# A graph kernel on one core: one of eight edge selections built on POOL, table and weight work cut into more pieces, the last empty half round dropped

## The reference, cut to what matters

```python
col = edge_index[1]
agg = jax.ops.segment_sum(edge_attr, col, num_segments=x.shape[0])
h = jnp.concatenate([x, agg], axis=-1)
h = jax.nn.relu(h @ W1 + b1)
h = jax.nn.relu(h @ W2 + b2)
h = h @ W3 + b3
...
deg = jax.ops.segment_sum(jnp.ones_like(src, dtype=x.dtype), src, num_segments=n)
```

## Time and profile before

| | us |
|---|---|
| median of 3 runs (2772.12 to 2778.86) | 2774.24 |
| the profiled execution's own time | 2776.76 |
| its span | 2775.0 |
| PE busy over the span | 2137.8 |
| DVE busy | 1990.9 |
| ACT busy | 1713.1 |
| POOL busy | 1795.3 |
| mean granted TensorE clock | 0.922 of full speed |

### The profile page before, as it was taken

How to read it: one execution, slowest core, us unless ns; L and a number is a source line. 1 busy time by engine, 2 the same in 40 slices (tenths; PEclk the granted TensorE clock), 3 DMA queues, 4 the chain that set the end, 5 groups by cost and what they waited for, 6 DMA issues and landing times. The chain is left out here.

```text
span 2775.0 us, 60619 instructions
## 1 busy us (share of the span) xinstructions
PE 2137.8 (77%) x13885; PEld 1762.5 (64%) x13886; DVE 1990.9 (72%) x7056; ACT 1713.1 (62%) x4484; POOL 1795.3 (65%) x1900
## 2 busy tenths in 40 slices
PE   6989977766787788788787876677788777777776
PEld 6988933254666676676676654566566666666655
DVE  7888868756777777777787855666676666676664
ACT  5766656455566666666676635556666666666663
POOL 1240055477777777777777726777777777777773
PEclk9999978689999989999999987999999999999998
DMA  6776623233334433434434413333333333333332
GB/s 185 237 243 184 205 65 110 89 103 105 110 112 117 119 113 116 119 114 117 118 112 120 117 56 97 107 109 111 107 113 111 106 110 110 108 110 110 106 113 59
DMA packets 183239, 331.21 MB, mean 119 GB/s; under 512 B 39636, under 2 KB 94887, under 8 KB 182964
## 3 DMA queue, kind: packets, MB, share of 16 engines
q0 software_dynamic: 82704, 223.04, 28.1%
q1 hardware_dynamic: 99524, 104.49, 12.3%
q10 hardware_dynamic: 736, 0.93, 0.1%
HBM read 295.96 MB, written 20.71 MB: 114 GB/s over the span
## 5 line engine op out<-in xcount | busy, mean ns | idle before, releaser
L1827 POOL DMA_INDIRECT arena<-kv_rows,idx_stage x1664 | 1618.5, 973 | 574.7 <-issue 498.4
L1915 PE MATMUL bank<-arena 128*128 128x136 f32 x3328 | 601.0, 313 | 315.5 <-DVE aggregate L1954 314.6
L1915 PEld LDWEIGHTS bank<-arena 128*128 128x128 f32 x3328 | 474.2, 204 | 423.5 <-DVE aggregate L1954 304.0
L1954 DVE TENSOR_TENSOR aggregate<-bank,aggregate 128x136 f32 x1664 | 489.5, 294 | 198.6 <-issue 99.0
L1906 PE MATMUL bank<-queries,arena 128*128 x3328 | 489.8, 294 | 133.1 <-DVE arena L1982 131.9
L1906 PEld LDWEIGHTS bank<-queries,arena 128*128 128x128 f32 x3328 | 437.0, 205 | 170.9 <-issue 170.3
L1982 DVE TENSOR_TENSOR arena<-bank,arena 128x512 f32<-128x512 f32 x416 | 286.4, 688 | 352.0 <-DMA arena<-kv_rows,idx_stage 278.3
L1848 ACT ACTIVATE arena<-iota_n,at_negdst 128x128 f32<-128x128 f32 x1664 | 527.4, 394 | 3.9 <-DMA queries<-arena 2.1
L1872 ACT ACTIVATE arena<-arena 128x32 f32<-128x32 f32 x416 | 93.6, 225 | 486.6 <-DVE arena L2012 304.7
L1891 PE MATMUL bank<-ident,arena 128*128 128x128 f32 x1664 | 273.6, 290 | 68.5 <-issue 37.2
L1962 DVE TENSOR_TENSOR arena<-arena 128x512 f32<-128x512 f32 x416 | 284.3, 683 | 46.1 <-ACT arena L1872 45.5
(11 more groups left out here) (279 smaller groups left out, 2699.4 us busy)
## 6 DMA issues: line engine op xcount, KB each, us to landing
arena<-in_edge_attr_dram SPq DMA_DIRECT2D x248, 256.0 KB, 3.2
arena<-kv_rows,idx_stage POOLq DMA_INDIRECT x1664
kv_rows<-arena SPq DMA_DIRECT2D x12, 512.0 KB, 3.8
kv_rows<-arena SPq DMA_DIRECT2D x24, 256.0 KB, 2.1
arena<-in_x_dram SPq DMA_DIRECT2D x12, 256.0 KB, 4.0
x_rows<-arena SPq DMA_DIRECT2D x12, 256.0 KB, 3.1
x_stream<-arena SPq DMA_DIRECT2D x12, 256.0 KB, 2.3
queries<-arena SPq DMA_DIRECT2D x12, 256.0 KB, 2.7
```

Source lines behind the costliest of these rows:

```text
L1827: pool.indirect_dma_start(kv[:, n, :], None, kv_dram[l], bass.IndirectOffsetOnAxis(idx_stage[:, half % 2, n:n + 1], 0)).then_inc(Z.kv_in[s ...
L1915: pe.matmul(sums_of(j), sel[:, r % SEL_SLOTS, j, :], msg[:, r % 2, j, :], start=True, stop=True).then_inc(Z.sum, 1)
L1954: dve.tensor_tensor(a, sums_of(j), a, ALU.add).then_inc(Z.added, 1)
```

## The change

Four edits. (1) Slot 0 of every odd round is selected by POOL, with four `tensor_scalar` is_equal of 128x128 in place of DVE's one 128x512; DVE keeps slots 0 and 1 of even rounds and slot 1 of odd rounds, ACT keeps slots 2 and 3. PE waits for `es_sel_pool` there. (2) Stops stand before each of the bodies 2 to 28. The step marks go to bodies 4 and 5, the tiles to 7, the ordering is halved (13, 14), the weight pieces go to 16, 18, 20, 22, their last part to 23, the table's parts to 24, 26, 28; PE's pieces to 3, 6, 12, 17, 19, 21, 25, 27. (3) POOL's loads and gathers are handed out over bodies 2 to 19, ahead of its selection for that body. (4) The last round (61) has no sums: 244 steps are done in 61 rounds; its counts stay.

```diff
-DVE_SLOTS = 2
-ACT_SLOTS = ES_SLOTS - DVE_SLOTS
+ES_DONE = ES_STEPS - ES_SLOTS
+assert ES_DONE >= ES_TILES + NT - 1
+POOL_ODD = 0
+DVE_SLOTS = ((0, 1), (1,))
+DVE_BODY = 3
+ACT_SLOTS = 2
+ACT_FIRST = ES_SLOTS - ACT_SLOTS
...
-        STOPS = tuple(range(3, 17, 2)) + tuple(range(17, 27))
+        STOPS = tuple(range(2, 29))
...
-                for n in range(2 * ES_SLOTS):
+                for n in range(ES_SLOTS if last else 2 * ES_SLOTS):
                     if not first:
                         sp.wait_ge(es_summed, (i - 1) * 2 * ES_SLOTS + n + 1)
...
+        def pool_edge_sums(pool):
+            pool.wait_ge(s_tab, 1)
+
+            def body(i):
+                m, s = i * 2 + 1, POOL_ODD
+                if i:
+                    pool.wait_ge(es_summed, (m - 2) * ES_SLOTS + s + 1)
+                for j in range(ES_SUB):
+                    one = pool.tensor_scalar(es_sel[:, 1, s, j, :], iota_n[:, :], es_dst[:, m * ES_SLOTS + s, j:j + 1], None, ALU.is_equal)
+                one.then_inc(es_sel_pool, 1)
+
+            def between(i):
+                if i == 2:
+                    pool_load_first(pool)
+                if i in range(3, 8):
+                    pool_load_layers(pool, i - 3)
+                if i == 8:
+                    pool_gather_rows(pool, AT, range(0, 4))
+                if i == 9:
+                    pool_gather_rows(pool, AT, range(4, AT.step_chunks))
+                if i in range(10, 15):
+                    pool_load_layers(pool, i - 5)
+                if i == 12:
+                    pool_write_pairs(pool)
+                if i == 15:
+                    pool_gather_pairs(pool, range(0, 4))
+                if i == 16:
+                    pool_gather_pairs(pool, range(4, AT.step_chunks))
+                if i == 18:
+                    pool_gather_in_order(pool, range(0, 4))
+                if i == 19:
+                    pool_gather_in_order(pool, range(4, AT.step_chunks))
+            for i in range(ES_BODIES - 1):
+                between(i)
+                body(i)
...
-                    for s in range(ES_SLOTS):
+                    for s in range(0 if last_body and h == 1 else ES_SLOTS):
                         pe.wait_ge(es_in[h * ES_SLOTS + s], 16 * (i + 1))
-                        if s < DVE_SLOTS:
-                            pe.wait_ge(es_sel_dve, m * DVE_SLOTS + s + 1)
+                        if h == 1 and s == POOL_ODD:
+                            pe.wait_ge(es_sel_pool, i + 1)
+                        elif s in DVE_SLOTS[h]:
+                            pe.wait_ge(es_sel_dve, i * DVE_BODY + h * len(DVE_SLOTS[0]) + DVE_SLOTS[h].index(s) + 1)
...
-                for h in range(2):
-                    m, ahead = i * 2 + h, not (last and h == 1)
...
+                for h in range(1 if last else 2):
+                    m = i * 2 + h
...
                     add(m, h, 1)
-                    for s in range(2):
-                        if ahead and s < DVE_SLOTS:
-                            select(m + 1, 1 - h, s)
-                        add(m, h, 2 + s)
+                    ahead = () if last else DVE_SLOTS[1 - h]
+                    for s in range(2, ES_SLOTS):
+                        if s - 2 < len(ahead):
+                            select(m + 1, 1 - h, ahead[s - 2])
+                        add(m, h, s)
...
-                if n == 1:
-                    dve_done(dve, AT)
...
+                if i == 4:
+                    dve_done(dve, AT, 0, 4)
+                if i == 5:
+                    dve_done(dve, AT, 4, AT.chunks)
...
+                if i in (13, 14):
+                    dve_order_steps(dve, i - 13)
+                if i in (16, 18, 20, 22):
+                    dve_weights(dve, (i - 16) // 2)
+                if i == 23:
+                    dve_weights(dve, 4)
+                if i in (24, 26, 28):
+                    dve_attention_table(dve, (i - 24) // 2)
...
-            sp.wait_ge(es_added, ES_STEPS)
+            sp.wait_ge(es_added, ES_DONE)
```

More of the change, by code:

```diff
@@ L438, in pool_load_weights @@
                           (rows_l[l][:, 1, :], w["b2"].partition_broadcast(P))]
-                for o, i in loads:
-                    pool.dma_start(o, i).then_inc(s_wl, 16)
+            n = -(-len(loads) // LOAD_PARTS)
+            for o, i in loads[part * n:(part + 1) * n]:
+                pool.dma_start(o, i).then_inc(s_wl, 16)
         def pool_prepare(pool):
@@ L623, in dve_order_steps @@
-            dve.tensor_reduce(rank, less, AX_X, ALU.add)
-            link(dve, dve.tensor_tensor(part, less, rows(count), ALU.mult))
-            link(dve, dve.tensor_reduce(start, part, AX_X, ALU.add))
-            dve.tensor_tensor(end, start, count, ALU.add)
-            link(dve, dve.tensor_tensor(shift, first, start, ALU.subtract))
-            inside, below = (g[:, 0:AT.step_chunks * FULL].rearrange("p (k u) -> p k u", u=FULL) for g in grid)
-            n = AT.step_chunks
-            dve.tensor_tensor(inside, columns(AT.step_id), rows(start, n), ALU.is_ge)
@@ L632, in dve_order_steps @@
-            link(dve, dve.tensor_tensor(below, columns(AT.step_id), rows(end, n), ALU.is_lt))
-            link(dve, dve.tensor_tensor(inside, inside, below, ALU.mult))
-            link(dve, dve.tensor_tensor(inside, inside, rows(shift, n), ALU.mult))
-            link(dve, dve.tensor_reduce(order_f, inside, AX_X, ALU.add))
-            dve.tensor_tensor(order_i, order_f, AT.step_id, ALU.add).then_inc(s_order, 1)
-            link(dve, dve.tensor_tensor(less, rows(rank), columns(units), ALU.is_equal))
@@ L639, in dve_order_steps @@
-            link(dve, dve.tensor_tensor(part, less, rows(units), ALU.mult))
-            link(dve, dve.tensor_reduce(key, part, AX_X, ALU.add))
-            dve.tensor_scalar(unit_base[0:1, 0:FULL], key[0:1, :], float(DUO), None, ALU.mult).then_inc(s_order, 1)
+            if half == 0:
+                dve.wait_ge(s_ahead, 1)
+                dve.memset(first[:, 0:1], 0.0)
+                link(dve, dve.tensor_copy(first[:, 1:FULL], bank[:, AHEAD_BANK, 0:FULL - 1]))
+                link(dve, dve.tensor_tensor(count, bank[:, AHEAD_BANK, 0:FULL], first, ALU.subtract))
+                link(dve, dve.scalar_tensor_tensor(out=key, in0=count, scalar=float(DUOS), in1=units, op0=ALU.mult, op1=ALU.add))
+                link(dve, dve.tensor_tensor(less, rows(key), columns(key), ALU.is_lt))
+                dve.tensor_reduce(rank, less, AX_X, ALU.add)
+                link(dve, dve.tensor_tensor(part, less, rows(count), ALU.mult))
+                link(dve, dve.tensor_reduce(start, part, AX_X, ALU.add))
+                dve.tensor_tensor(end, start, count, ALU.add)
+                link(dve, dve.tensor_tensor(shift, first, start, ALU.subtract))
@@ new lines, in dve_order_steps @@
+            if half == 1:
+                inside, below = (g[:, 0:AT.step_chunks * FULL].rearrange("p (k u) -> p k u", u=FULL) for g in grid)
+                n = AT.step_chunks
+                dve.tensor_tensor(inside, columns(AT.step_id), rows(start, n), ALU.is_ge)
+                link(dve, dve.tensor_tensor(below, columns(AT.step_id), rows(end, n), ALU.is_lt))
+                link(dve, dve.tensor_tensor(inside, inside, below, ALU.mult))
+                link(dve, dve.tensor_tensor(inside, inside, rows(shift, n), ALU.mult))
+                link(dve, dve.tensor_reduce(order_f, inside, AX_X, ALU.add))
+                dve.tensor_tensor(order_i, order_f, AT.step_id, ALU.add).then_inc(s_order, 1)
+                link(dve, dve.tensor_tensor(less, rows(rank), columns(units), ALU.is_equal))
+                link(dve, dve.tensor_tensor(part, less, rows(units), ALU.mult))
+                link(dve, dve.tensor_reduce(key, part, AX_X, ALU.add))
+                dve.tensor_scalar(unit_base[0:1, 0:FULL], key[0:1, :], float(DUO), None, ALU.mult).then_inc(s_order, 1)
@@ L825, in sp_edge_sums, with body @@
             sp.wait_ge(s_start_in, 1)
-            def body(i, first):
+            def body(i, first, last):
                 _, starts = nc.values_load_multi_w_load_instructions(
```

147 lines of the change are left out of this document (70 added, 77 removed).

## The result

| | before | after |
|---|---|---|
| median of 8 runs, us | 2773.16 | 2764.40 (2758.99 to 2766.86) |
| the profiled execution / its span, us | 2776.76 / 2775.0 | 2764.31 / 2762.5 |
| ahead of the edge stage | 35.3 | 35.8 |
| edge stage, first count group to the end of the last | 305.6 | 289.7 |
| dense stage, to POOL's first gather of attention | 213.8 | 218.5 |

The ratio is 0.9966, interval 0.9957 to 0.9975: 8.8 us less, outside the 0.3% only just, where the forecast had 9.5 less. The edge stage is 15.9 us shorter; it began 0.5 later and so ended 15.4 earlier (325.47 in place of 340.91). The dense stage took 4.7 back.

The account below looks back on a forecast made before the run. PE was taken to bound quiet edge rounds, losing time to DVE's long pieces. Gains of 6 us from waits, clock and loads and 3.5 from the last round took 2774.2 to 2764.7, say 2765; range 2755 to 2783.

Parts of the forecast that it names:

- faster by a little: Whole kernel: main case with 0 to 0.6 us of blocks a body, 2760 to 2767 us, chance 0.44.
- What bounds the kernel: Edge stage: PE bounds quiet rounds at 8.82 us a body; some 22 us of waits, clock and late loads can be had.
- The last round, 3.5: End of edge stage: without sums, the last count group follows directly, 4.41 - 0.91 = 3.5 us less.
- POOL's instruction and its blocking: Edge stage: POOL's four selection instructions take 0.30 us each and stop DVE for 0.4 us a body.
- I take 0.30: Price of one POOL selection instruction in us, between rows of 0.28 and 0.76.
- each stops DVE for t less 0.2: Each POOL selection instruction hides 0.2 us under a DVE add and stops DVE for the rest: 0.4 us a body.
- slower rival: Edge stage: POOL's blocking makes DVE the bound; at 0.76 us an instruction +21 us, 2795; chance 0.16.
- The list of pieces: Edge stage: PE's loss to DVE's cut and moved pieces, body by body, together 13.5 us in place of 14.4 + 1.3.
- no blocking: Rival: POOL never stops DVE; list 12.8 us with clock, total -12.5, 2762; with full clock, 2755 to 2762, chance 0.13.
- POOL's queue, 0: Edge stage: POOL's loads and gathers ahead of its selection cost PE nothing; uncovered, 2 us at each of six bodies.
- Time before the end of the edge stage moves everything behind it: Whole kernel: only the edge stage's end can move, so its 9.5 us come off the total.
- a rival's threshold: Edge stage: from 0.57 us a POOL instruction, DVE needs longer than PE in every body and becomes the bound.

Follow-up runs that it names:

- e2: Kernel before with only the last round's sums left out; 2775.98 us, ratio 1.001; edge stage 302.3 in place of 305.6.
- e6: Changed kernel with POOL's four selection instructions done twice, first into a spare buffer; 3579.8 us, ratio 1.0007.
- e4: Changed kernel with a two-input 128x512 add on POOL ahead of its selection, into a spare buffer; 3569.05 us, ratio 0.9982.
- e3: Changed kernel with step marks, ordering and last weight piece made whole again, POOL's selection kept; 2773.59 us, ratio 0.9997.
- e1: Changed kernel with slot 0 of odd rounds selected by DVE again, the other three edits kept; 2766.94 us, ratio 0.9978.
- e0: Changed kernel run once more, unchanged; 2767.35 us, ratio 0.9977 to the kernel before.
- e5: Changed kernel with marks at 3, 4, 5, ordering in four, table and POOL's later gathers one body later; 3563.93 us, ratio 0.9963.
- e7: Changed kernel with 12 one-column clears on DVE ahead of the edge stage; second chip group, 3560.69 us, ratio 0.9955.
- e11: Kernel before with 95 one-column clears on DVE in its start, dense loop at instruction 1079; 3584.77 us, ratio 1.0014.
- e10: Changed kernel with 12 one-column clears on DVE, same kernel as e7 run again; 3556.93 us, ratio 0.9940.
- e8: Kernel before without the last round's sums, plus ten one-column clears on DVE in its start; 3583.64 us, ratio 1.0022.
- the finer cut: Changed kernel with marks in three, ordering in four, table and later gathers one body later; run twice, 3563.93 and 3559.33 us, ratios 0.9963 and 0.9943.

## Why the prediction was right, and where its terms were not

The forecast was 9.5 us less and the likeliest case was "faster by a little"; 8.8 it was. That the number came out so near is luck. The edge stage, the only one that was to move, gained 15.9 and not 9.5, and 4.7 in the dense stage and some 2 behind it were given back.

1. **What bounds the kernel** held. Quiet bodies stayed at 8.82, and the gain in the edge stage came out of PE's waits for DVE and of the clock.

2. **The last round, 3.5.** The edge stage shows it: 3.3 in e2, 3.6 in after by the same reckoning (4.41 less the 0.8 that the run of 26 lasts longer than one group).

3. **POOL's instruction and its blocking: the step that failed.** "I take 0.30" was 0.85, and 0.59 in e6 where DVE stood idle beside it, so the nearest row was the one above (0.76, fp32) and not the one in bf16. And "each stops DVE for t less 0.2" was wrong by more: 0.03 a body in place of 0.4. With the measured t the rule gives 4 x 0.65 = 2.6 us a body, which is beyond the slower rival's 2.24; by that rival's own sum it is some 32 us slower. Both errors together brought me near the truth; the rule alone, with a good price, would have forecast a loss. The row behind it is an add over 128x512 that was running when DVE's operation came, and e4 shows the rule sound for that: 0.57 us a body. I carried it over to four short instructions with one tensor input, where no row spoke. The Trainium skill (SBUF — State Buffer, Who interferes with whom) says that a DVE instruction with two SBUF inputs contends with a GpSimd instruction that reads SBUF. The trace agrees that the two contend, for e4's add and for the selection; what I had wrong is who pays. For the selection POOL does: 92 DVE selections at 684 ns beside 120 of POOL's at 848, and 1.04 us for those of POOL's that overlap DVE most. For the add it is mostly whoever starts second, as e4's 28 and 20 operations show. Why POOL's selection never stops DVE isn't shown: it differs from the add in inputs, in length and in operation, and none of the three was varied alone. The number of inputs alone can't be the reason, since the two-input product at 372.67 gave way too.

4. **The list of pieces.** This is therefore the "no blocking" case: 12.8 forecast for it, clock included, 11.2 measured. Body by body, forecast (with blocking) and measured: ordering 1.9 and 4.1 against 2.11 and 4.92, where the 4.92 has 1.6 of clock in it (forecast 2.0, apart); marks 0.75 and 0.8 against 0 and 0.17; counts 0.65 against 0; weights 1.15, 0.8, 1.55 and the table 1.8 against 0.53, 1.2, 0.95 and 1.29. The small pieces cost less than forecast. The likely reason, an estimate: without the blocks there is more air, and the tolerance grew by about the 0.95 us of a slot's 8 records that go ahead (1.13 less the overlap of a modelled end; 3.82 / 4), where I had put 0.60, the width of the selection; the ordering doesn't, since two pieces of 4.0 and 5.15 in successive bodies exceed any air.

   e3 (+6.0) and e1 (+5.4 to 7.8) show that each edit is worth its while when the other is there. Of the stage's 15.9 the last round has 3.3 (e2). Cutting with the selection left on DVE gives 305.6 - 297.5 - 3.3 = 4.8. The selection with whole pieces gives 305.6 - 298.1 - 3.3 = 4.2, or 6.5 without the 2.3 us for which e3's body 2 waited for edge rows, as e0's did and after's didn't. Both together give 12.6. In e1 and e3 alike POOL's loads are handed out, and body 12, where edge rows landed late before, grows by 0.2 in place of 1.8. So cutting has some 3, the selection 5, the loads 1.6, and about 3 come only with both; beside a scatter of 2 us from profile to profile that last figure is weak. The handing out of the loads was never tried alone.

5. **POOL's queue, 0.** Right: PE never waited for it. The queue wasn't far from its end, though: the nearest that POOL came was 3.7 us ahead of PE, and with 3.4 us more a body e6 loses 15.5.

6. **Not foreseen: 4.7 us given back in the dense stage.** "Time before the end of the edge stage moves everything behind it" was the step. DVE's standstill of 3.5 and 1.0 us came in after, e0, e3, e4 and e6, and never in before, e1, e2, e5, e7 to e11. From the end of the loop's branch to DVE's next instruction 3.8 to 4.5 us pass in those five kernels, and 0.26 to 0.30 in the other nine. In the five, three transfers of 8 KB of the kind "instruction" run in the 8 us behind the branch, in the nine none: DVE goes on 1.3 to 1.6 us after the first has landed, and ends its second stop 1.25 to 1.3 us after the second. The transfers don't name their engine, but with times that repeat so closely DVE was waiting for its code. Twelve clears (e7, e10) take the wait away with no other work changed, so it hangs on where DVE's code lies, not on the data or the order of work. The Trainium skill (Runtime: NRT & Kernel Launch, Instruction fetch mechanics) says that a taken branch to outside the pages at hand makes an engine wait for its code; the trace agrees for the first stop, which stands behind a branch with code being loaded in it. The second, eight instructions on in a straight run, has a transfer of code too, but no branch. Which placements are bad stays open, as e11, with the loop at the same count, has no stop; the price (4.5 us) and a cure (another placement) are shown.

With these the sum is: stage -15.9, a start 0.5 later, dense +4.7, so -10.7 for after, against -8.8 of the medians. **The rest is open.** To compare the part behind the dense stage I take each profile's rest less what that execution lies above its median: before 2216.8, after 2218.6, e0 2221.0, e1 2218.7, e2 2223.1, e3 2217.4. It scatters by 6 us between kernels that don't differ there, and before has the lowest: of the gain, 0.6 to 6.3 us don't arrive. For e2 that is all of it. Code has a share in this too: in attention DVE stops behind 14 more loop branches in every kernel, each time some 3 us and with a transfer of code in the stop, 42.5 us in all before, 41.5 after and 45.4 in e2. Whether these stops lie on the path isn't shown, and e8 couldn't tell. Nor was the exchange of one resource tried alone (POOL's selection on the kernel before).

On a version that beats both: on the second group of chips the finer cut is 0.4 to 0.6% below before, but so is the changed kernel with twelve clears, within each other's intervals, though the finer cut's edge stage is 4.3 to 5.0 shorter. Neither ran beside the plain changed kernel. The shorter stage is shown, a shorter kernel over after isn't.

## What to carry to other kernels

Where an engine makes single long detours, the loss is lag plus piece above a tolerance: shorten the piece and widen the air between two. Here both paid. Cutting pays only where the parts come under what the air can drain: the marks, in parts of 3.0 and 1.85 us, gained 3.2, the ordering, in parts of 4.0 and 5.15, gained 1.1, and in four parts (e5) 4.2 more. When a rival's threshold decides the sign, price it by a row of the same operation, size and type, or say that its condition itself is unproven: here the threshold was passed and nothing happened. And a stage that ends 15 us sooner is not a kernel that does; cut the trace into stages with fixed ends before believing either, and where an engine stops for nothing behind a branch, look whether code is being loaded.

## What the runs showed of the hardware that was not expected

- GpSimd's `tensor_scalar` is_equal over 128x128 fp32 takes 0.59 us at best and 0.85 beside a busy DVE, and leaves DVE's two-input operations at their length (684 against 681 ns, 815 against 814). A two-input add over 128x512 takes 1.15 us and costs DVE 0.57; when DVE was first, it is mostly the add that waits (1.50 to 1.94 in five of 30).
- VectorE stood still for 3.5 and 1.0 us behind a loop's branch in the dense stage while three 8 KB transfers of code ran, and twelve more instructions at 10 us, over 400 us earlier, took that away. In attention it stops so for some 3 us behind each of 14 branches.
- TensorE fell to the lower clock after waits of 2.85 and 3.01 us (e1: 32 records in 6.60 and 5.44 us in place of 3.82), and after 2.30 (e3) and 2.58 with a short group behind them. A wait of 1.37 with the same short group left it full in after, e0 and e10 and lowered it in e7, where 1.85 left it full: the length of the wait alone doesn't decide. A wait cut from 7.3 to 2.6 still cost 1.6 us of clock.
